# Expert outputs added into the output by the scatter itself, one q projection with shuffles, and VectorE's copy of h

## What is computed

```python
h = tok(x, W0, b0, pos0, W1, b1, pos1, W2, b2, pos2, scale_emb)   # (16, 221, 128)
h = h + attn(layernorm(h), w_qkv, w_agg, b_agg)                   # 8 heads of 16
h = h + ffn(layernorm(h), expert_weights, expert_indices, w1, w2)

# ffn: only the first 1024 rows (tokens) have experts; each has two assignments of 8 experts
y = gelu(x[token] @ w1[e]) @ w2[e]          # for every assignment, sorted by expert
out[token] += weight * y                    # both assignments of a token are added
```

## Time and profile before

| | |
|---|---|
| median of 3 runs | 271.49 us (271.13 to 271.51) |
| profiled execution: time, span | 271.6 us, 270.0 us |
| PE (TensorE matmul) busy | 255.9 us, 95% |
| PEld (TensorE weight load) busy | 222.1 us, 82% |
| DVE (VectorE) busy | 211.9 us, 78% |
| ACT (ScalarE) busy | 143.3 us, 53% |
| POOL (GpSimd) busy | 114.9 us, 43% |
| mean granted TensorE clock | 0.991 of full speed |

### The profile page before, as it was taken

One profiled execution on the slowest core, in us unless ns is written; L12 is line 12 of the kernel. 1 busy time (PEld: TensorE's weight loads), 2 busy tenths in 40 slices (PEclk: granted clock), 3 DMA queues, 4 the chain that ended last, 5 costly groups with the idle time before them and its releaser, 6 DMA issues.

```text
span 270.0 us, 7288 instructions
## 1 busy us (share of the span) xinstructions
PE 255.9 (95%) x2925; PEld 222.1 (82%) x2925; DVE 211.9 (78%) x453; ACT 143.3 (53%) x223; POOL 114.9 (43%) x178
## 2 busy tenths in 40 slices
PE   8999989999899999999998999999999999998991
PEld 8899977879697979797977979888888888887771
DVE  2976489879989878898968869696969697877684
ACT  4770332725251615252447676777768585869240
POOL 4000031203348474747573546656474838353200
PEclk9999999999999999999999999999999999999996
DMA  6999200089100000000021102011111111000252
GB/s 210 417 389 438 125 1 2 0 277 301 48 24 14 23 14 26 13 27 9 28 51 30 47 12 54 30 40 39 40 39 43 40 30 39 13 26 31 84 143 85
DMA packets 15623, 22.29 MB, mean 83 GB/s; under 512 B 2415, under 2 KB 10327, under 8 KB 15559
## 3 DMA queue, kind: packets, MB, share of 16 engines
q1 hardware_dynamic: 13447, 18.67, 21.1%
q0 software_dynamic: 1760, 2.60, 3.1%
q10 hardware_dynamic: 384, 0.57, 0.7%
HBM read 17.43 MB, written 5.95 MB: 87 GB/s over the span
## 4 chain that ended last, share of the span: by engine, by line
PE 70%; DVE 15%; ACT 6%; issue 4%; DMA 2%; POOL 1%; SPq 0%; DVEq 0%; POOLq 0%; ACTq 0%
PE e_ps L1153 11%; PE s_ps L1239 11%; PE s_ps L1153 8%; PE e_ps L1435 7%; PE m_ps L1353 7%; PE m_ps L1420 5%; PE m_ps L1224 5%; DVE nmax L903 4%; ACT L668 3%; PE e_ps L1420 3%; PE m_ps L1214 3%; DMA x_raw<-x 2%; PE m_ps L1383 2%; DVE x_lo L790 2%; PE m_ps L1203 1%
## 5 line engine op out<-in xcount | busy, mean ns | idle before, releaser
L903 DVE TENSOR_REDUCE nmax<-s_ps 128x4 fp32r<-128x884 f32 (+1 forms) x60 | 61.8, 1070 | 15.5 <-PE s_ps L1239 14.8
L620 ACT ACTIVATE probs<-s_ps 128x888 f32<-128x888 f32 (+1 forms) x60 | 51.4, 910 | 23.2 <-PE s_ps L1239 23.2
L517 POOL DMA_INDIRECT y_rows<-y_sb,idx_u x23 | 23.1, 1003 | 28.4 <-PE s_ps L1239 25.6
L462 POOL TENSOR_TENSOR var_eps<-mv,eps_t 128x2 f32<-128x2 f32 x16 | 5.6, 350 | 68.8 <-DVE mv L862 68.8
L495 POOL DMA_INDIRECT z_slots<-z,slot_u x20 | 23.4, 1170 | 15.8 <-PE s_ps L1239 11.4
L1353 PE MATMUL m_ps<-probs,v_aug 128*32 128x221 f32 (+1 forms) x480 | 25.8, 353 | 0.0
L1435 PE MATMUL e_ps<-w_now,hidT 128*128 128x128 f32 x184 | 23.2, 275 | 0.0
L1435 PEld LDWEIGHTS e_ps<-w_now,hidT 128*128 128x128 f32 x184 | 22.4, 192 | 0.1
L604 ACT COPY zT<-m_ps 128x221 f32<-128x221 f32 x16 | 5.5, 344 | 30.0 <-PE m_ps L1204 30.0
L1239 PE MATMUL s_ps<-k_a,q_hi 32*128 32x222 f32 (+1 forms) x252 | 19.1, 309 | 2.0 <-DVE nmax L903 1.1
L1153 PE MATMUL e_ps<-x_hi,w_hi 128*128 128x252 f32 (+2 forms) x128 | 20.7, 294 | 0.1
(11 more groups left out here) (169 smaller groups left out, 613.9 us busy)
## 6 DMA issues: line engine op xcount, KB each, us to landing
w_raw<-wt SPq DMA_DIRECT2D x6, 512.0 KB, 10.1
x_raw<-x SPq DMA_DIRECT2D x6, 512.0 KB, 10.5
w_sb<-w SPq DMA_DIRECT2D x1, 2048.0 KB, 9.9
z_slots<-z SPq DMA_DIRECT2D x1, 1518.0 KB, 13.8
zs<-z_slots SPq DMA_DIRECT2D x7, 198.0 KB, 2.6
x_raw<-x SPq DMA_DIRECT2D x4, 256.0 KB, 5.5
out<-h SPq DMA_DIRECT2D x11, 64.0 KB
c_sb<-consts SPq DMA_DIRECT2D x1, 599.5 KB, 13.2
```

The costliest lines, as they stand in the source:

```text
L517: g.indirect_dma_start(y_dram, bass.IndirectOffsetOnAxis(ap=idx_u[:, at:at + 1], axis=0), y_sb[:, n % 2, i, :], None).then_inc(y_out[n % 2 ...
L620: s.activation(probs[0:n, blk, 2 * f:2 * f + 2].rearrange("p t u n -> p t (u n)"), s_ps[0:n, 2 * f:2 * f + 2, 0:2 * NE], ACT.Exp, scale=DH ...
L903: v.tensor_reduce(nmax[0:n, blk, 2 * f:2 * f + 2, DH:DH + 2], src, AX_X, ALU.max, negate=True).then_inc(max_ready, 1)
```

## The change

The results of the experts are no longer kept in a tensor of their own. SP stores `h1k` of batch b in cycle b + 1, and each `scatter_y` is an indirect DMA that adds its rows onto those of `out` in DRAM. So that no two additions meet on a row, every scatter waits until the one before has landed, and the first until all of `h1k` is stored. A token whose two assignments have the same expert would stand twice in one scatter: `route_pairs`, new on VectorE in cycle -2, adds both weights into the first and gives the second the number of no token. Such slots, and the empty ones, go to rows of the last batch, which is stored after all scatters. `load_y`, `combine` and the late stores of `h1k` are gone.

From batch 8 on q is projected once (one matmul of two instructions, with a sixth block of weights), and VectorE doubles it with two stream shuffles into `q_d` in SBUF; the high and low parts are taken from there. `project_v` then waits for the shuffles, not for `q_low`. On ScalarE `q_high` moves behind `k_high`, on VectorE `q_low` and `ln_stats` behind `k_low`. The copy of v goes from VectorE to ScalarE from batch 8 on.

From cycle 7 on VectorE copies h out of PSUM (`late_h_copy`), between `take_max` and the shuffles. From cycle 8 on `ln_z(c + 1)` stands between the two `maxima`, and `z_turn(c + 1)` behind `s1(c, 1)`.

```diff
+DOUBLED = 8
+LATE_Z = 9
+TWICE = tuple([DH * u + i % DH for i in range(32)] for u in range(2))
...
+        def q_src(b):
+            return q_d[:] if b >= DOUBLED else m_ps[:, 0, 0:2 * N].rearrange("p (u n) -> p u n", u=2)
...
+        rows = out.rearrange("b n d -> (b n) d")
...
+            def store_h1k(b):
+                sp.wait_ge(h1_ready, b + 1)
+                sp.dma_start(out[b][0:N0, :], h1k[:, b, 0, :]).then_inc(first_stored, 16)
+                sp.dma_start(out[b][N0:N, :], h1k[0:N1, b, 1, :]).then_inc(first_stored, 16)
...
             def store_h1(b):
                 sp.wait_ge(h1_ready, b + 1)
+                if b == BATCH - 1:
+                    for i in range(2):
+                        sp.wait_ge(y_out[i], 16 * sum(ROUND_TILES[i::2]))
...
-                if c == BATCH - 1:
-                    load_y()
-                if c == BATCH:
-                    for t in (1, 0):
-                        sp.wait_ge(combined[t], (2, 4)[t])
-                        for lo, hi in SPANS[t]:
-                            sp.dma_start(out[0:FFN_B].rearrange("b n d -> n b d")[P * t + lo:P * t + hi],
-                                         h1k[lo:hi, :, t, :]).then_inc(final_out, 16)
+                if 0 < c <= FFN_B:
+                    store_h1k(c - 1)
...
+                if i:
+                    pool.wait_ge(y_out[n % 2], 16 * (sum(ROUND_TILES[n % 2:n:2]) + i))
+                elif n:
+                    pool.wait_ge(y_out[(n - 1) % 2], 16 * sum(ROUND_TILES[(n - 1) % 2:n:2]))
+                else:
+                    pool.wait_ge(first_stored, 32 * FFN_B)
                 at = TILES_BEFORE[n] + i
-                g.indirect_dma_start(y_dram, bass.IndirectOffsetOnAxis(ap=idx_u[:, at:at + 1], axis=0),
-                                     y_sb[:, n % 2, i, :], None).then_inc(y_out[n % 2], 16)
+                g.indirect_dma_start(rows, bass.IndirectOffsetOnAxis(ap=idx_u[:, at:at + 1], axis=0),
+                                     y_sb[:, n % 2, i, :], None, compute_op=ALU.add).then_inc(y_out[n % 2], 16)
...
+                if b >= DOUBLED:
+                    act.wait_ge(q_d_ready, 2 * (b - DOUBLED) + 2)
+                else:
+                    act.wait_ge(q_done, b + 1)
+                s.copy(q_hi[:, b % 2, :, 0:N], q_src(b)).then_inc(q_hi_ready, 1)
...
                 gelu(n, 0)
                 if c - 1 >= 0 and n != 0:
                     o_raw_copy(c - 1)
+                if LATE_Z <= c + 1 < BATCH:
+                    zT_copy(c + 1)
...
                 if experts:
                     load_table(ACT.Exp)
-                if experts and c + 2 < BATCH:
-                    h_copy(c + 2)
-                if 0 <= c + 1 < BATCH:
+                if 0 <= c + 1 < DOUBLED:
...
                 if 0 <= c + 1 < BATCH:
                     k_high(c + 1)
+                if DOUBLED <= c + 1 < BATCH:
+                    q_high(c + 1)
                 if n == ROUNDS - 1:
                     last_y(0)
                 if 0 <= c < BATCH:
                     exps(c, 1)
+                if DOUBLED <= c + 1 < BATCH:
+                    late_v_copy(c + 1)
                 if n == ROUNDS - 1:
-                    last_v_copy(c + 1)
                     last_y(1)
 
 
...
+            def route_pairs():
+
+                dve.wait_ge(ew_in, 16)
+                ids = c_sb[:, C_IDS:C_IDS + COLS].rearrange("p (j k) -> p j k", k=TOP_K)
+                e = ei_f[:].rearrange("p (j k) -> p j k", k=TOP_K)
+                v.tensor_copy(ids_t[:], ids)
+                link(v.tensor_tensor(same[:], e[:, :, 0], e[:, :, 1], ALU.is_equal))
+                v.tensor_scalar(same_id[:], same[:], NO_TOKEN, None, ALU.mult)
+                link(v.tensor_tensor(same_w[:], same[:], ew_sb[:, :, 1], ALU.mult))
+                v.tensor_tensor(ew_sb[:, :, 0], ew_sb[:, :, 0], same_w[:], ALU.add)
+                link(v.tensor_tensor(ew_sb[:, :, 1], ew_sb[:, :, 1], same_w[:], ALU.subtract))
+                v.tensor_tensor(ids_t[:, :, 1], ids_t[:, :, 1], same_id[:], ALU.add).then_inc(pairs_ready, 1)
...
+            def late_h_copy(b):
+                dve.wait_ge(h_turned, b + 1)
+                dve.wait_ge(hb_ready, b)
+                dve.wait_ge(z_ready, 2 * b)
+                v.tensor_copy(h_sb[:], m_ps[:, 1, 0:2 * P].rearrange("p (t d) -> p t d", t=2)).then_inc(h_ready, 1)
...
+            def q_double(b):
+                dve.wait_ge(q_done, b + 1)
+                for u in range(2):
+                    v.stream_shuffle(q_d[:, u, :], m_ps[:, 0, 0:N], TWICE[u]).then_inc(q_d_ready, 1)
...
-                v.tensor_copy(idx_u[:, TILES_BEFORE[n]:TILES_BEFORE[n + 1]], zs[:, 0:m, ID]).then_inc(idx_ready, 1)
+                v.tensor_scalar(idx_u[:, TILES_BEFORE[n]:TILES_BEFORE[n + 1]], zs[:, 0:m, ID], c_sb[:, C_FREE:C_FREE + 1], None,
+                                ALU.min).then_inc(idx_ready, 1)
...
                 if n == 0:
                     zsT_evac(0)
+                if c + 1 >= LATE_Z and c + 1 < BATCH:
+                    ln_z(c + 1)
                 if 0 <= c < BATCH - 1:
                     maxima(c, 1)
                 if c == BATCH:
                     nmaxT_copy(c)
                 elif c >= 0:
                     take_max(c)
+                if 0 <= n and c + 2 < BATCH:
+                    late_h_copy(c + 2)
+                doubled = DOUBLED <= c + 1 < BATCH
+                if doubled:
+                    q_double(c + 1)
                 if c - 1 >= 0:
                     turn(c - 1)
                 if c == BATCH - 1:
                     zsT_evac(n + 1)
                 if c - 1 >= 0:
                     norm(c - 1)
-                if 0 <= c + 1 < BATCH:
+                if 0 <= c + 1 < BATCH and not doubled:
                     q_low(c + 1)
-                if c + 2 < BATCH:
+                if c + 2 < BATCH and not doubled:
                     ln_stats(c + 2)
                 if c == 0:
                     route_slots()
                 if 0 <= c + 1 < BATCH:
                     k_unit(c + 1)
                     k_low(c + 1)
-                if c + 2 < BATCH:
+                if doubled:
+                    q_low(c + 1)
+                    if c + 2 < BATCH:
+                        ln_stats(c + 2)
+                if c + 2 < min(LATE_Z, BATCH):
                     ln_z(c + 2)
                 if c == -2:
                     route_tiles()
+                    route_pairs()
                     lo_x(6)
                 if n == 2:
                     v.tensor_copy(sel_r[:].rearrange("p u n -> p (u n)"), c_sb[:, C_SEL:C_UP]).then_inc(consts_r, 1)
-                if 0 < c + 1 < BATCH - 1:
+                if 0 < c + 1 < DOUBLED:
                     v_copy(c + 1)
                 if c == 1:
                     lo_x(8)
                 if c == 2:
                     lo_x(9)
-                if c == BATCH - 1:
-                    for t in (1, 0):
-                        combine(t, 0)
-                        combine(t, 1)
...
-                for u in range(2):
-                    mm = pe.matmul(m_ps[:, 0, u * N:(u + 1) * N], wqkv_sb[:, u, :], zT[:], start=True, stop=True)
+                if b >= DOUBLED:
+                    mm = pe.matmul(m_ps[:, 0, 0:N], wqkv_sb[:, 5, :], zT[:], start=True, stop=True)
+                else:
+                    for u in range(2):
+                        mm = pe.matmul(m_ps[:, 0, u * N:(u + 1) * N], wqkv_sb[:, u, :], zT[:], start=True, stop=True)
                 mm.then_inc(q_done, 1)
 
...
 
-                pe.wait_ge(q_ready, b + 1)
+                if b >= DOUBLED:
+                    pe.wait_ge(q_d_ready, 2 * (b - DOUBLED) + 2)
+                else:
+                    pe.wait_ge(q_ready, b + 1)
...
                 p1, p2, pm, p3, p4 = PLAN.get(c, (0, 0, 0, 0, 0))
                 if here:
                     s1(c, 0)
-                if ahead1:
+                if ahead1 and c + 1 < LATE_Z:
                     z_turn(c + 1)
                 if n > 0:
                     hidden(n, 0)
                 tok_some(p1)
                 if here:
                     s1(c, 1)
+                if ahead1 and c + 1 >= LATE_Z:
+                    z_turn(c + 1)
```

More of the change, by code:

```diff
@@ L60 @@
 ID, WEIGHT = P, P + 1
-SPANS = (((0, N0),), ((0, 80), (80, N1)))
+NO_TOKEN = 4096.0
 E0 = 7
@@ L113 @@
 C_UP = C_SEL + 2 * P
-C_END = C_UP + 1
+C_FREE = C_UP + 1
+C_END = C_FREE + 1
 def piece_cols(piece):
@@ L215, in build @@
         idx_u = sb("idx_u", [P, N_TILES], U32)
+        ids_t = sb("ids_t", [P, FJ, TOP_K])
+        same = sb("same", [P, FJ])
+        same_id = sb("same_id", [P, FJ])
+        same_w = sb("same_w", [P, FJ])
         ei_sb = sb("ei_sb", [P, FJ, TOP_K], I32)
@@ L336, in build @@
         y_out = [sem(f"y_out{i}") for i in range(2)]
-        combined, final_out = [sem(f"combined{t}") for t in range(2)], sem("final_out")
+        first_stored, pairs_ready = sem("first_stored"), sem("pairs_ready")
         block = ctx.enter_context(nc.Block())
```

(18 more changed lines are left out.)

37 lines of the change are left out of this document (10 added, 27 removed).

## The result

The changed kernel takes 274.35 us (median of 4 runs, 274.23 to 276.01); the kernel before took 271.46 beside it (271.13 to 271.51). The ratio is 1.0126, with a 95% interval of 1.0110 to 1.0142: slower, as forecast, but by 2.9 and not by 0.9. The profiled execution took 274.41, with a span of 272.6.

A forecast was written before the change was run, and what follows sets the result against it. TensorE's own order of work was taken as the bound, with one stall at project_k. Terms +0.47 +0.32 +2.04 +0.13 -1.43 -0.60 = +0.93 gave 272.5 us against the profiled 271.6, 272.4 as median; 8-in-10 range 269.8 to 275.0.

The forecast's parts named there:

- beginning: Cycle -2: route_pairs adds seven small VectorE operations, together 1.0 us, of which +0.47 comes through.
- cycle 7: Shorter project_q gives nothing here; h's copy and shuffles move `down`'s weights from 148.88 to 149.20: +0.32 us.
- cycles 8 to 13: Stall moves from project_k to `down`, which waits for zsT; each cycle 0.34 us longer, six of them: +2.04.
- cycle 14: VectorE and ScalarE are the path; s1's second block 0.34 earlier, q_low behind k_low 0.50: +0.13 us.
- residual without combines: At the end, batch 14's residual starts right behind its aggregate, at 261.64 in place of 263.07: -1.43 us.
- clock in the last aggregate: Last aggregate, moved to 264.3, runs before the clock falls, in half the time: -0.60 us; otherwise 0.
- ln_z now runs between the two maxima, where VectorE idles over 1: In cycles 8 to 13, late ln_z fits VectorE's idle time, its rstd ready some 2.5 us before; no cost.
- The shuffles ahead of zsT: Two VectorE shuffles, 0.38 us each, delay zsT, so `down` waits; each of cycles 8 to 13 0.34 longer.
- Rival A: VectorE's shuffles are cheap, 0.25 us each: total -0.9, 270.6 us; chance 0.20.
- B: `down` doesn't wait for zsT, as turn and copy overlap more: total -5.3, 266.2 us; chance 0.07.
- D: VectorE's shuffles are dear, 0.50 us each: total +2.6, 274.1 us; chance 0.10.
- C: Adding scatters chain up on GpSimd, from landings of 4.75 us each on; at 5.2, 277.7 us; chance 0.13.

The follow-up runs named there:

- w2_later: Changed kernel with GpSimd's w2 copies behind the cycle's first result scatter in place of ahead of it; 272.15 us, ratio to before 1.0033.
- scatter_only: Kernel before with only the experts' part of the change (adding scatters, route_pairs, early h1k stores); q, h, z as before; 271.01 us, ratio 0.9994.
- zst_first_w2_later_slots_last: Changed kernel with zsT ahead of shuffles and turn, w2 copies behind the first scatter, slot_w and idx_u copies behind norm; 270.61 us, ratio 0.9980.
- no_doubling_slots_last: Changed kernel with q projected twice, VectorE copying v, w2 copies behind the first scatter, zsT ahead of turn, small copies behind norm; 268.90 us, ratio 0.9915.
- all_repairs: Changed kernel with zsT ahead of shuffles and turn, w2 copies behind the first scatter, and route_pairs in cycle 1; 276.16 us, ratio 1.0195.
- no_scatter_change: Kernel before with only the q, h and z part of the change; experts' rows keep their own tensor and combines; 274.01 us, ratio 1.0106.
- zst_first: Changed kernel with the evacuation zsT ahead of the two shuffles and the turn on VectorE; 271.08 us, ratio to before 1.0002.
- no_doubling_w2_between: As no_doubling_slots_last, but GpSimd's w2 copies stand ahead of the first result scatter, which waits for a landing; 267.90 us, ratio 0.9875.
- scatter_only_plain: As scatter_only, but the chained scatters write plainly instead of adding, so output rows are overwritten; 270.57 us, ratio 0.9978.

## Why the prediction was right in sign and wrong in size

| step | predicted | measured |
|---|---|---|
| beginning | +0.47 | +0.60, and 0.07 more up to cycle 7 |
| cycle 7 | +0.32 | +0.16 |
| cycles 8 to 13 | +2.04 | +3.08 |
| cycle 14 | +0.13 | +0.31 |
| residual without combines | -1.43 | -1.42 |
| clock in the last aggregate | -0.60 | -0.47 |
| last store's issue to the end of the span | 0 | +0.20 |
| outside the span | 0 | +0.28 |
| sum | +0.93 | +2.8 |

The measured ones are differences of the first maxima's starts, of the residual's start, of the last aggregate's start to the last store's issue (1.58 before, 1.11 after), and of that issue to the end of the span (2.73 and 2.93). The text of the prediction counts seven equal cycles, 8 to 14; there are six, and cycle 14 took 11.72 before. Its sum counts them rightly.

VectorE's first maxima, behind which z was to go, and GpSimd's w2 copies, in cycle 10 of the kernel before:

```profile
182.15 2.06 DVE L903 TENSOR_REDUCE nmax<-s_ps 128x4 fp32r<-128x884 f32 x2
```

```profile
183.15 1.72 POOL L539 COPY w_now<-w_sb 128x512 f32 x3
```

- **The step that failed** is "ln_z now runs between the two maxima, where VectorE idles over 1", at no cost. I looked at VectorE's idle time and at when rstd is ready, and not at what another engine does to the same memory in that time. The trace of before has the w2 copies at 183.15 to 184.87, just where z was to go (the rows above). The term was 0.43 to 0.46 in each of cycles 9 to 11, 0.33 in 12 and in 13, and 0.24 in 14 (after against w2_later): 2.2 in all.
- **The shuffles ahead of zsT.** The mechanism holds: `down` waits for zsT, project_k for nothing. Its size was too large: w2_later has +0.17 for my +0.34. A shuffle is 0.41 long, but 0.31 from start to start, where I took 0.38; two are 0.14 of the difference of 0.17. Against that, `down`'s weights follow zsT's end by 0.11, where I took 0.04. The permutation's own instruction, for which the prediction cites the Trainium skill, is there, and takes 0.01 and not the 0.06 to 0.10 that I would have given it. At 0.31 my own sum broke even; w2_later, with the z term out, came to 272.15. That it is near the 272.4 is partly chance, as the terms of the beginning and the end were off the other way.
- **Rival A** (cheap shuffles, 0.25) was no further from the 0.31 than my 0.38, and its result was wrong, for z's sake. **B** is excluded by the 0.64 before `down`. **D** by 0.41 of length. **C** didn't occur in the changed kernel: landings of 3.4 are near my 3.5, scatter_only has one long cycle. But its threshold was drawn too simply. With faster cycles a landing of 4.88 (zst_first_w2_later_slots_last) or two of 4.18 and 4.29 in a row (no_doubling_slots_last) delayed what GpSimd has behind the scatter, and two or three operations on two engines further the cycle was longer by 1.7 and 1.0.
- **Beginning.** The seven small operations take 0.93 from 36.39 to 37.32, within 1.0 as worked out; 0.60 comes through, since z there waits 0.29 for its rstd, for which it didn't wait before. In all_repairs, with them in cycle 1, the first maxima start at 41.47, but the third at 70.11 as in the changed kernel (70.10): cycle 1 has no room either.
- **Combines and clock** came as the rows said. That the stretch behind the last store's issue takes 0.20 longer was not looked for. Of it 0.04 lies ahead of the end of SP's last wait and 0.16 behind, among the instructions that close the program. All variants with the chained scatters, the plain ones too, have the 0.16; no_scatter_change hasn't. Why stays open, as do the 0.28 outside the span.

## What to carry to other kernels

An engine's idle slot isn't free for any operation: before moving a VectorE copy, tensor_scalar or two-input operation within SBUF, look at what GpSimd does in SBUF in that stretch, and put GpSimd's copies beside VectorE's reductions and evacuations from PSUM. Follow such a collision when it is "repaired" by a move, because it passes on to the next operation of that kind, and a three-element copy can hold a whole queue for 2 us. And price an operation that doesn't wait by the distance from start to start of its like.

## What the runs showed of the hardware

- VectorE's operations of 0.1 to 0.4 took up to 2.05 beside GpSimd's copies, which start 0.56 apart; one wait can span several copies in a row. In all_repairs slot_w, begun at 174.84 beside the first copy, ended at 176.89, 0.03 behind the third. GpSimd's times are rough in a trace. In zst_first the first of the two z operations started at 183.65, when GpSimd was in an adding scatter (183.32, 1.62 long) and the copies (184.40) had not begun, and ended at 185.66, 0.09 behind the first copy. A z that started 0.87 to 0.97 into such a scatter, with no copy behind, took 0.59 and 0.60 (w2_later, 185.31; no_doubling_w2_between, 183.39). Whether an early part of the scatter holds it, or the copy that came later was let in first, stays open.
- The three w2 copies themselves take 2.28 right behind an adding scatter and 1.72 behind a plain one (scatter_only, without z beside them, has 2.26 to 2.28; no_scatter_change, with it, 1.72); where GpSimd waited 1.24 between an adding scatter and them, they took 1.97 (no_doubling_w2_between).
- With the adding scatters GpSimd's queue moved its 2.60 MB in 4336 packets (scatter_only), with plain ones in 1760 (scatter_only_plain).
- Beside the copies, operations that read PSUM kept their time: a pair of maxima 2.05 to 2.06, a shuffle 0.40 to 0.41 (all_repairs, 177.36 and 177.67).
- The clock was still at 2.4 GHz after TensorE had been idle for 1.36; before, it had fallen in an idle time of 2.78.
